# Longer rings for the gathered rows in three edge stages: 8, 6 and 8 rounds in place of 4

## The reference

```
# layer "L0_ffn", on its own edge list: scores of 4 heads without types
e = leaky_relu(a_src[src] + a_dst[dst], 0.2)
e_max = segment_max(e, dst)
ee = exp(e - e_max[dst])

# layer "L1_gnn", 50,000 edges of 8 types
aw_q_edge = q_att[etype, col_idx]
msg_edge  = v_msg[etype, row_idx]
attn_score = sum(aw_q_edge * k[row_idx], axis=-1)

# layer "L3_gnn", the weighted sum
msg = edge_weight[:, None] * h[edge_col]
z = segment_sum(msg, edge_row)
```

## Time and profile before

| | us |
|---|---|
| median of 3 runs (6537.68 to 6546.70) | 6540.89 |
| the profiled execution, its own time | 6548.93 |
| its span from the first to the last instruction | 6547.3 |
| `gat_s`, start of the first gather to start of the last maximum | 1341.6 to 1812.7 |
| `hgt_s`, the same | 2638.9 to 3382.6 |
| `wsum_a`, start of the first gather to start of the last sum | 5629.4 to 6248.2 |
| POOL busy in the whole span | 2429.1 (37%) |
| PE, DVE busy in the whole span | 4610.8 (70%), 3512.4 (54%) |

### The profile page before, as it was taken

How to read it: one execution, slowest core, us unless ns; L and a number is a source line. 1 busy time by engine, 2 the same in 40 slices (tenths; PEclk the granted TensorE clock), 3 DMA queues, 4 the chain that set the end, 5 groups by cost and what they waited for, 6 DMA issues and landing times. The chain is left out here.

```text
span 6547.3 us, 89145 instructions
## 1 busy us (share of the span) xinstructions
PE 4610.8 (70%) x23040; PEld 3253.1 (50%) x23041; DVE 3512.4 (54%) x7298; ACT 1668.6 (25%) x3845; POOL 2429.1 (37%) x2714
## 2 busy tenths in 40 slices
PE   5866769734449969455657889998999495344558
PEld 1213435533347734344435577776777353344446
DVE  8988983645582345577766843342111323544543
ACT  0944543411102224011100133333222121100022
POOL 0848855555508733555520000001111201467610
PEclk8988999855559989677667989999999697677779
DMA  0002447411110038777755510003333321223210
GB/s 29 2 10 101 155 157 239 128 27 27 25 59 21 8 128 334 252 243 243 247 168 187 193 22 10 14 5 122 103 104 105 88 98 50 72 89 91 89 28 20
DMA packets 392065, 669.88 MB, mean 102 GB/s; under 512 B 115851, under 2 KB 280850, under 8 KB 387242
## 3 DMA queue, kind: packets, MB, share of 16 engines
q1 hardware_dynamic: 295938, 420.30, 19.8%
q0 software_dynamic: 95744, 247.14, 12.6%
q10 hardware_dynamic: 192, 0.15, 0.0%
HBM read 438.59 MB, written 228.81 MB: 102 GB/s over the span
## 5 line engine op out<-in xcount | busy, mean ns | idle before, releaser
L3367 POOL CAST sagel_piece<-x 128x1600 fp32r<-128x1600 f16 (+1 forms) x75 | 112.4, 1499 | 1582.4 <-DMA x<-counts 1140.0
L1072 POOL DMA_INDIRECT wsum_a_rows<-table,edge_src x416 | 426.5, 1025 | 273.5 <-issue 111.2
L1086 PE MATMUL wsum_a_ps<-wsum_a_hot,wsum_a_rows 128*128 128x128 f32 x1664 | 293.8, 352 | 330.0 <-DVE big L1113 253.7
L2172 POOL DMA_INDIRECT big<-hgt_table,edge_key x416 | 393.2, 945 | 351.0 <-DVE hgt_s_tmp L2259 200.0
L555 POOL DMA_INDIRECT back_sorted<-back_space x391 | 404.0, 1033 | 245.9 <-POOLq L1758 175.5
L1086 PEld LDWEIGHTS wsum_a_ps<-wsum_a_hot,wsum_a_rows 128*128 128x128 f32 x1664 | 275.6, 260 | 348.1 <-DVE big L1113 267.1
L3423 PE MATMUL sagel_ps<-sagel_piece,sagel_high 128*128 128x512 f32 (+1 forms) x1050 | 400.0, 388 | 0.8 <-issue 0.8
L555 POOL DMA_INDIRECT own_sorted<-big x256 | 275.9, 1078 | 311.5 <-issue 310.6
L767 PE MATMUL cnt_ps<-cnt_hot_s,cnt_hot_d 128*128 128x512 bf16 x1760 | 318.2, 334 | 94.8 <-DVE cnt_hot_s L749 89.2
L3423 PE MATMUL sagel_ps<-sagel_piece,sagel_low 128*128 128x512 f32 (+1 forms) x1050 | 380.7, 376 | 0.0
L2220 PE MATMUL hgt_s_pq<-big 128*128 x1248 | 249.0, 373 | 181.9 <-DVE hgt_s_tmp L2259 111.8
(11 more groups left out here) (977 smaller groups left out, 10887.2 us busy)
## 6 DMA issues: line engine op xcount, KB each, us to landing
hgt_edge_values<-big SPq DMA_DIRECT2D x104, 512.0 KB
big<-hgt_edge_values SPq DMA_DIRECT2D x104, 512.0 KB, 3.5
x<-counts SPq DMA_DIRECT2D x75, 400.0 KB, 3.1
x<-counts SPq DMA_DIRECT2D x75, 384.0 KB, 3.0
counts<-big SPq DMA_DIRECT2D x25, 832.0 KB
counts<-big SPq DMA_DIRECT2D x25, 768.0 KB
big<-counts SPq DMA_DIRECT2D x30, 640.0 KB
counts_turned<-big SPq DMA_DIRECT2D x30, 640.0 KB
```

The source lines that it names most:

```text
L1072: nc.gpsimd.indirect_dma_start(rows[n % DEEP][:, u, :], None, table, bass.IndirectOffsetOnAxis(ap=e.src[:, g:g + 1], axis=0)).then_inc(gat ...
L1086: mm = nc.tensor.matmul(ps[r.slot % 2][u][:, k * P:(k + 1) * P], rows[r.slot][:, u, k * P:(k + 1) * P], hot[r.slot % 2][:, u, :], start=Tr ...
L2172: nc.gpsimd.indirect_dma_start(rows[n % DEEP][:, u, :], None, at.table, bass.IndirectOffsetOnAxis(ap=at.index[:, g:g + 1], axis=0)).then_i ...
```

## The change

`places` and the two stage functions take the length of the ring of gathered rows from the stage: 8 in `gat_s` and `wsum_a`, 6 in `hgt_s`, whose ring spreads into half of a third buffer. All else keeps its length: `ends` and `hot_t` stay at four slots, `hot`, `tmp` and the PSUM tiles at two. The loop bodies of PE, DVE and ACT grow with it: from four rounds to eight in `wsum_a` and `gat_s` and to twelve in `hgt_s` (the least common multiple of 6 and 4). Fourteen more semaphores are cleared by POOL at the ends of `gat_s` (4) and `hgt_s` (10).

```diff
-        self.n, self.slot, self.turn = j * DEEP + c, c % DEEP, j + c // DEEP
+        self.n, self.slot = j * unroll + c, c % DEEP
...
+    def turn(self, ring):
+        return self.j * (self.unroll // ring) + self.c // ring
...
-def rolling(eng, step, rounds):
+def rolling(eng, step, rounds, unroll):
+    times = (rounds - 5) // unroll
     for c in range(-2, 3):
-        step(Round(0, c, rounds, False))
-    with eng.Fori(0, rounds // DEEP - 2) as j:
-        for k in range(DEEP):
-            step(Round(j, 3 + k, rounds, True))
-    for c in range(rounds - 5, rounds + 3):
-        step(Round(0, c, rounds, False))
+        step(Round(0, c, rounds, False, unroll))
+    with eng.Fori(0, times) as j:
+        for k in range(unroll):
+            step(Round(j, 3 + k, rounds, True, unroll))
+    for c in range(3 + times * unroll, rounds + 3):
+        step(Round(0, c, rounds, False, unroll))
...
 def aggregate_t
+    RING = 8
-        rows = [c.enter_context(nc.sbuf_tensor(f"{nm}_rows{a}", [P, R, W], F32)) for a in range(DEEP)]
+        rows = [c.enter_context(nc.sbuf_tensor(f"{nm}_rows{a}", [P, R, W], F32)) for a in range(RING)]
-                    if n >= DEEP:
-                        pool.wait_ge(multiplied, (n - DEEP + 1) * R)
+                    if n >= RING:
+                        pool.wait_ge(multiplied, (n - RING + 1) * R)
-                rolling(pe, step, rounds)
+                rolling(pe, step, rounds, RING)
...
 def edge_scores
+    RING = at.ring
+    UNROLL = math.lcm(RING, DEEP)
-        rows, ends, hot_t = at.places(WR, P // 2, P // 2)
+        rows, ends, hot_t = at.places((WR, RING), (P // 2, DEEP), (P // 2, DEEP))
-        spread_ends, gathered, stored = (gather_sems(nc, nm, x, DEEP) for x in ("ends_in", "gathered", "stored"))
+        gathered = gather_sems(nc, nm, "gathered", RING)
+        spread_ends = sems(nc, c, nm, " ".join(f"ends_in{u}" for u in range(DEEP)))
+        stored = sems(nc, c, nm, " ".join(f"stored{u}" for u in range(RING if at.put_by is not None else 0)))
-                    if n >= DEEP:
-                        pool.wait_ge(mixed, n - DEEP + 1)
+                    if n >= RING:
+                        pool.wait_ge(mixed, n - RING + 1)
                         if at.put_by is not None:
-                            pool.wait_ge(stored[n % DEEP], 16 * (n // DEEP))
+                            pool.wait_ge(stored[n % RING], 16 * (n // RING))
                         else:
-                            pool.wait_ge(kept, n - DEEP + 1)
+                            pool.wait_ge(kept, n - RING + 1)
-                rolling(pe, step, rounds)
+                rolling(pe, step, rounds, UNROLL)
...
-                               spare=[b3], held=held)
+                               spare=[b3], ring=8, held=held)
...
-                           [q01[:, :, 0:D], q01[:, :, D:], q2], H, DK, dots=True, spare=[b1, b2], put_by=put_by)
+                           [q01[:, :, 0:D], q01[:, :, D:], q2], H, DK, dots=True, spare=[b1, b2, b4[:, NT * D // 2:]], ring=6,
+                           put_by=put_by)
```

More of the change, by code:

```diff
@@ L1 @@
+import math
 from contextlib import ExitStack
@@ L1079, in step @@
                     if r.there:
-                        pe.wait_ge(gathered[r.slot], (r.turn + 1) * 16 * R)
+                        pe.wait_ge(gathered[r.c % RING], (r.turn(RING) + 1) * 16 * R)
                         pe.wait_ge(matched, r.n + 1)
@@ L1995, with __init__, places @@
 class EdgeAttention:
-    def __init__(self, edges, index, table, key_at, value_at, q, heads, dv, dots, spare, held=None, put_by=None):
+    def __init__(self, edges, index, table, key_at, value_at, q, heads, dv, dots, spare, ring, held=None, put_by=None):
         self.edges, self.index, self.table, self.q = edges, index, table, q
         self.key_at, self.value_at, self.heads, self.dv, self.dots = key_at, value_at, heads, dv, dots
-        self.spare, self.held, self.put_by = spare, held, put_by
-    def places(self, *widths):
+        self.spare, self.ring, self.held, self.put_by = spare, ring, held, put_by
+    def places(self, *wanted):
         left = [[buf, 0] for buf in self.spare]
         def take(width):
-            place = next(p for p in left if p[1] + R * width <= NT * D)
+            place = next(p for p in left if p[1] + R * width <= p[0].shape[1])
             place[1] += R * width
             return place[0][:, place[1] - R * width:place[1]].rearrange("p (r w) -> p r w", r=R)
-        return [[take(width) for _ in range(DEEP)] for width in widths]
+        return [[take(width) for _ in range(count)] for width, count in wanted]
 def make_pick(nc, kit, link, space):
@@ L2153, in _ @@
                     if at.put_by is not None:
-                        sp.wait_ge(gathered[n % DEEP], (n // DEEP + 1) * 16 * R)
+                        sp.wait_ge(gathered[n % RING], (n // RING + 1) * 16 * R)
                         sp.dma_start(at.put_by[:, n * R:(n + 1) * R, :],
-                                     rows[n % DEEP][:, :, at.value_at:at.value_at + HV]).then_inc(stored[n % DEEP], 16)
+                                     rows[n % RING][:, :, at.value_at:at.value_at + HV]).then_inc(stored[n % RING], 16)
                 if at.put_by is not None:
-                    for u in range(DEEP):
-                        sp.wait_ge(stored[u], 16 * (rounds // DEEP))
+                    for u in range(RING):
+                        sp.wait_ge(stored[u], 16 * -(-(rounds - u) // RING))
             @block.gpsimd
@@ L2181, in step @@
                         if at.held is not None:
-                            act.wait_ge(gathered[r.slot], (r.turn + 1) * 16 * R)
+                            act.wait_ge(gathered[r.c % RING], (r.turn(RING) + 1) * 16 * R)
                             nc.scalar.copy(at.held[:, ds(r.n * R, R), :],
-                                           rows[r.slot][:, :, at.value_at:at.value_at + HV]).then_inc(kept, 1)
+                                           rows[r.c % RING][:, :, at.value_at:at.value_at + HV]).then_inc(kept, 1)
                         act.wait_ge(scored, r.n + 1)
@@ L2252, in step @@
                     if r.there:
-                        mine, key = tmp[r.slot % 2][:], rows[r.slot][:, :, at.key_at:at.key_at + WT]
+                        mine, key = tmp[r.slot % 2][:], rows[r.c % RING][:, :, at.key_at:at.key_at + WT]
                         dve.wait_ge(spread, r.n + 1)
@@ L2257, in step @@
                         if at.dots:
-                            dve.wait_ge(gathered[r.slot], (r.turn + 1) * 16 * R)
+                            dve.wait_ge(gathered[r.c % RING], (r.turn(RING) + 1) * 16 * R)
                             nc.vector.tensor_tensor(mine, key, pq_v, ALU.mult).then_inc(mixed, 1)
@@ L2282, in step @@
                     if far.there:
-                        dve.wait_ge(spread_ends[far.slot], (far.turn + 1) * 16)
+                        dve.wait_ge(spread_ends[far.slot], (far.turn(DEEP) + 1) * 16)
                         if far.looped or far.c >= DEEP:
@@ L2557, in edge_sums @@
         region, = many(1, "region", [1, groups], I32)
-        rows, = at.places(HV)
+        rows, = at.places((HV, DEEP))
         ps = c.enter_context(nc.psum_tensor(f"{nm}_ps", [P, 2 * REGION], F32))
```

25 lines of the change are left out of this document (12 added, 13 removed).

## The result

| | before | changed | ratio, 95% interval |
|---|---|---|---|
| median, us | 6541.37 | 6594.44 | 1.0082, 1.0065 to 1.0100 |

The change costs 53 us; the forecast was +17 us. The time lies 6 us inside the range that was given for all rivals together, 6500 to 6600, and outside the forecast's own, 6546 to 6576. The profiled execution of the changed kernel took 6605.02 us (span 6603.4). Behind the change in the code L2172 became L2181, L2197 L2206, L2183 L2192, L2249 L2258, L2259 L2268, L1072 L1078, L1086 L1092 and L1102 L1108.

The account below looks back on a forecast made before the run. PE's signals, held while POOL issues gathers, were taken to bound the three stages. 7.3 (gat_s) + 6.3 (hgt_s) + 10.4 (wsum_a) - 8 + 1 = +17 us on 6540.9 gave 6558; range 6500 to 6600, the forecast's own 6546 to 6576.

Parts of the forecast that it names:

- Start of the stages: POOL's first run lengthens by the added slots while consumers stand still: +20.0 us gat_s, +10.0 hgt_s, +20.0 wsum_a.
- End of the stages: After POOL's last round more rounds remain, run at the fast rate: -12.7 us gat_s, -3.7 hgt_s, -9.6 wsum_a.
- Body of the stages: 0: Mid-stage, the cycle of 12.75 us is the consumers' and no ring length enters it: 0 us.
- PE waiting for rows: -8: In wsum_a, PE's 49.8 us of waits for gathered rows go, a sixth of it counted: -8 us.
- Semaphores: +1: Fourteen more clears by POOL at the barriers: +1 us, between 0 and 4.2.
- Loop bodies: 0: Fewer passes save a branch each and cost nothing if PE's 580-instruction loop stays in its instruction store: 0 us.
- PE's loop is fetched anew: Rival: PE's longer loops in hgt_s and gat_s fetch packets late each pass, 18 to 35 us, about 6585; chance 0.05.
- start and end cancel: Rival: single signals pass in the longer first run, stages regain at the end the start's loss; 6541 us; chance 0.20.
- the hold ends by itself: Rival: the hold doesn't grow with POOL's run, the start costs nothing, gains stay: -34 us, 6507; chance 0.15.
- pauses get rarer: Rival: one POOL pause for four rounds, not two, in gat_s and wsum_a: -88 us, about 6450; chance 0.10.
- longer holds in the middle: Rival: mid-wsum_a, POOL issues four more rounds before pausing, up to 20 us each run: +40 us, 6598; chance 0.10.
- The hold itself: In the three stages, PE's signals arrive late or not at all while POOL issues gathers, bursting when it pauses.

Follow-up runs that it names:

- e3_hgt4: On chip A, rings of 8 in gat_s and wsum_a, hgt_s kept at 4 rounds in ring and loop, against the kernel before: 6629.37 us, ratio 1.0041.
- e2_loops: On chip A, kernel before with all rings at 4 and only the loop bodies lengthened to 8, 12 and 8 rounds: 6605.61 us, ratio 0.9999.

## Why the prediction was nearly right, point by point

The offsets of single rounds against the stage's first gather, changed less before, on P, in us:

| | start: said, found (by round 20) | body | end | sum: said, found |
|---|---|---|---|---|
| gat_s | +20.0, +21.9 | 0, -1.2 | -12.7, -12.1 | +7.3, +8.6 |
| hgt_s | +10.0, +9.0 (round 14) | 0, +26.0 | -3.7, -2.9 | +6.3, +32.1 |
| wsum_a | +20.0, +22 | -8, -3.4 | -9.6, -9.6 | +2.4, +9.0 |

The parts hang on the round at which the table cuts a stage, as slots come free two rounds at a time. In hgt_s the rounds around the 14th give +9.0 to +13.5, so its body is +21 to +26. In wsum_a the offset swings between +13 and +29 in the body, so -3.4 there can't be told from 0 or from -8. The sums do not hang on it.

- **Start of the stages**: right in size in all three. Wrong in detail: POOL ran 12 and 10 rounds in gat_s and wsum_a, not 11 and 9, as one signal slips through within the run, and ACT's wait of 42 us came as two of 23 and 26. A held signal isn't always held to the end of the run, but the price is the same: 4.5 to 7 us for each slot added.
- **End of the stages**: right, within 1 us in each.
- **Body of the stages: 0**: right in gat_s (cycle 12.7 us) and the step that failed in hgt_s, the term that was mis-sized: +26 us. I had argued from gat_s's cycle that no length of the ring enters, and called it the cycle of the consumers. It isn't theirs: without gathers they need 7.1 us for two rounds of gat_s. The 12.7 us are POOL's issuing of two rounds, 9.7, and a stop of 3.0. In hgt_s on P the ring of 4 had let half of the cycles be short, 13.3 us in place of 14.5; with the ring of 6 a fifth were. How much of it is the ring's depends on the chip: on A the body took 7.33 and 7.38 us a round with 4 and 7.50 with 6, +9 to +13 us over 74 rounds. That short cycles are lost is shown by the traces of P; what decides between the two kinds is not. A stop of POOL's between the two rounds isn't enough: on A the ring of 4 had 18 such cycles of 14.83 us in e3_hgt4 and 7 of 13.87 in e2_loops.
- **PE waiting for rows: -8**: these waits fell by 27 us, and at most a few of them came through. That the rest went into POOL's refilling, as the prediction put it, is likely and not shown; the sixth that it took was a guess.
- **Semaphores: +1**: not seen. From the end of gat_s to the start of hgt_s, with four of the clears, it is 826.2 us before and 826.3 now; the stretch behind hgt_s, with the other ten, varies by 8 us among kernels without them.
- **Loop bodies: 0**: right, 0.9999 with the loops alone. The rival that PE's loop is fetched anew is out; by the Trainium skill's window of two pages (Runtime: NRT & Kernel Launch, Instruction fetch mechanics) the bodies of 580 instructions should have stalled in each pass, by its room for 2,048 instructions not, and the runs agree with the second (three packets in 655 us of hgt_s).
- **The rivals of the hold**: "start and end cancel" and "the hold ends by itself" fell with the starts of +22, +9 and +22; "pauses get rarer" with the unchanged 98.1 us in gat_s (its price there was set a little high: the earlier trace rows has 32 waits, not 36); of "longer holds in the middle" wsum_a shows none that counts (-3.4 in the body). That rival's time, 6598, came closest to the measured 6594. This is luck: its mechanism, four more rounds of POOL's in wsum_a before it pauses, is not what was found in hgt_s.
- **The hold itself.** That the gathers slow the consumers on A is shown by the run without them, and that it is PE's signals that come late by the trace: the matmul has ended up to 25 us before its signal is recorded. What about the gathers holds them was tried only where there is no hold. The same gathers in long runs show none of it on B to E, so POOL's run is a condition of it and not the whole cause. Two rivals are untested: that the hour and not the chip makes the difference, and that recording has a part in it. What speaks for the second is that where the signals are held, the trace also lacks 40% of DVE's and ACT's update records (1,637 of 2,715 are there in the three stages on P), while on B, and on A without gathers, it has them all.

In all, +17 fell 36 us short of +53: 26 in hgt_s, which the table finds in its body, 7 in wsum_a, 1 in gat_s, and the rest outside of the stages. The mechanism of the start and the end held; that the time is in the wide range is luck too, as the range reached that far only for the longer holds, at a chance of 0.10.

## What to carry to other kernels

A longer ring pays only for waits that end at the producer's next free slot while the consumer is fast. Before lengthening one, look at what the consumer does while the producer runs: where its signals come in bursts behind the producer's pauses, each slot costs its filling time at the start (5 us here) and gives back only the difference of the held to the free rate at the end (2 to 3 us). And a cycle that is worked out in one stage holds for that stage: read it again in each stage that the change touches. Last, take the profile of before on the chip on which the change is timed, and on a second one: here the same edit was +0.8% on one and -0.2% on another.

## What the runs showed of the hardware

- The same program takes 6541 us on P, 6606 on A and 6174 to 6187 on four others. Between A and B 388 of the 426 us lie in the three stages of gathers (474, 781 and 624 us on A in e2_loops, whose rings are those of before, against 371, 567 and 553), in runs of POOL's that are issued at the same 0.94 us a gather and 0.30 between them.
- On P and A, PE's `turned` and `multiplied` arrive up to some 25 us late while POOL issues gathers back to back; the burst comes 2 to 8 us after it stops. Two thirds of PE's recorded updates are late there (693 of 1,037 on P, 683 of 967 on A in e2_loops) and practically none of DVE's and ACT's. On B and C one of 1,106 and one of 1,113 is, and the longest wait of ACT for `turned` is 2.6 us in a run of POOL's of 360 us.
- On P, signals of PE are not late while POOL issues an indirect DMA every 1.52 us with a memset behind each and the DMA engines 5% busy (0 of 177), nor while the DMA engines are 67% busy without POOL (2 of 419). With the memsets and the DMA engines 77% busy 40 of 99 are, by up to 2.0 us; on B none of 127.
- PE's granted clock doesn't explain it: 0.50 in gat_s (its 1.2 GHz level) on P and on B, at 471 and 371 us. In hgt_s it is 0.69 on P and 0.81 on B, where it may follow the time or add to it.
